# A decoder layer on one core: the weights' preparation spread over the attention turns

## The reference

```python
x = LN(x + self_attention(x))            # 16 query heads, 4 key/value heads, head size 32
x = LN(x + cross_attention(x, ctx))      # 16 heads
amp = sigmoid(x @ amp_w + amp_b)
ph  = tanh(x @ ph_w + ph_b) * pi
h   = (cos(ph) + sin(ph)) * amp
for l in range(2):
    ent = (h @ ent_w[l] + ent_b[l]) @ ent_pw[l] + ent_pb[l]     # 512 -> 2048 -> 512
    h   = LN(h + ent) * g3[l] + b3[l]
    t   = h @ path_w[l][p] + path_b[l][p]                       # p = 0, 1
    h   = LN(h + sum_p t_p * (cos(phase[l][p]) + sin(phase[l][p]))) * g4[l] + b4[l]
out = LN(x + h)
```

## Time and profile before

| | us |
|---|---|
| median of 3 runs | 985.45 (985.22 to 986.75) |
| the profiled execution | 986.26 |
| its span, first to last instruction | 984.4 |
| self attention turns, to about | 258.6 |
| cross attention turns | 258.6 to 512.0 |
| flush, to the first instruction of the fusion phase | 512.0 to 535.4 |
| fusion phase and first gates, to the first drained feed forward unit | 535.4 to 691.2 |
| the rest | 691.2 to 984.4 |

### The profile page before, as it was taken

One profiled execution on the slowest core, in us unless ns is written; L12 is line 12 of the kernel. 1 busy time (PEld: TensorE's weight loads), 2 busy tenths in 40 slices (PEclk: granted clock), 3 DMA queues, 4 the chain that ended last, 5 costly groups with the idle time before them and its releaser, 6 DMA issues. The chain is left out here.

```text
span 984.4 us, 20365 instructions
## 1 busy us (share of the span) xinstructions
PE 891.6 (91%) x5900; PEld 739.3 (75%) x5900; DVE 724.3 (74%) x2072; ACT 528.6 (54%) x1640; POOL 430.6 (44%) x601
## 2 busy tenths in 40 slices
PE   4899999999888999999985987989999999999993
PEld 4788888888777788778864766667778778778672
DVE  3778888888877888888874687892756667657557
ACT  3756665566556666676661333335565564564461
POOL 0234334432222222222231797950664665565466
PEclk9899999999998999999997898999999999999997
DMA  4423332235623543445311764631101101001001
GB/s 148 142 86 109 113 117 89 82 123 166 186 73 109 140 124 95 136 125 139 93 53 41 251 235 161 213 106 65 44 1 43 43 0 43 0 0 43 1 1 43
DMA packets 67045, 92.97 MB, mean 94 GB/s; under 512 B 7216, under 2 KB 41008, under 8 KB 66608
## 3 DMA queue, kind: packets, MB, share of 16 engines
...
## 5 line engine op out<-in xcount | busy, mean ns | idle before, releaser
L675 ACT ACTIVATE prob<-bank,nmax 128x128 f32<-128x128 f32 (+1 forms) x512 | 207.1, 432 | 44.8 <-DVE nmax L734 44.2
L161 PE MATMUL bank<-w_ffn,hT 128*128 128x512 f32 x768 | 193.2, 403 | 0.0
L734 DVE CUSTOM_DVE_ANT_0 bank<-bank,mask 128x128 f32<-128x128 f32 (+1 forms) x512 | 164.1, 392 | 10.8 <-PE bank L895 10.5
L161 PEld LDWEIGHTS bank<-w_ffn,hT 128*128 128x128 f32 x768 | 141.8, 190 | 31.0 <-POOL hT L1366 0.2
L563 POOL TENSOR_SCALAR rwide<-rden 128x256 f32<-128x256 f32 x64 | 26.0, 406 | 275.4 <-DVE rden L745 275.4
L161 PE MATMUL bank<-xT,w_att 128*128 128x256 f32 x864 | 120.8, 293 | 15.4 <-DVE w_att L699 10.5
L161 PEld LDWEIGHTS bank<-xT,w_att 128*128 128x128 f32 x864 | 113.6, 198 | 21.1 <-DVE xT L722 7.0
L161 PE MATMUL bank<-tile 128*128 128x512 f32 x384 | 100.2, 415 | 19.4 <-DVE tile L1177 19.4
L675 ACT ACTIVATION_READ_ACCUMULATOR prob<-bank,nmax 128x1 f32 x512 | 111.6, 218 | 0.0
L907 PE MATMUL bank<-ident,prob 128*128 128x128 f32 x768 | 107.2, 277 | 1.8 <-DVE probT L741 1.4
L1438 ACT ACTIVATE ht<-bank,cols 128x128 f32<-128x128 f32 x192 | 72.3, 457 | 64.2 <-PE bank L1575 64.2
(11 more groups left out here) (119 smaller groups left out, 1472.5 us busy)
## 6 DMA issues: line engine op xcount, KB each, us to landing
q<-stage SPq DMA_DIRECT2D x192, 128.0 KB, 2.3
...
xT_raw<-in_xT SPq DMA_DIRECT2D x8, 512.0 KB, 4.1
xres<-in_x SPq DMA_DIRECT2D x8, 512.0 KB, 3.4
xb<-x SPq DMA_DIRECT2D x8, 512.0 KB, 4.5
aux<-in_path_w SPq DMA_DIRECT2D x8, 512.0 KB, 3.4
```

The lines of the kernel that those rows point to most:

```text
L161: ins = t.matmul(out, lhs(a, k), rhs(b, k), start=first and n == 0 and m == 0, stop=last and n == len(kts) - 1 and m == 2, skip_group_chec ...
L675: ins = s.activation(prob[:, u, c * width:(c + 1) * width], banks[u][:, c * width:(c + 1) * width], ACT.Exp, scale=-1.0, bias=nmax[:, i % ...
L734: ins = v.tensor_tensor_reduce(scored, scored, mask[:, S - width:S], scale=-1.0, scalar=3e38, op0=ALU.add, op1=ALU.min, accum_out=nmax[:, ...
```

## The change

The fusion phase is gone. Its work is in the attention phase:

- The product of the entity weights is cut into 64 units "fu", each for one block of 128 rows of the result and 256 of the 2048 inner columns: 6 matmuls of 512 columns (and one of the identity in the first unit of each sum). They are fillers of the cross turns: ten in the first, nine in each of the next six, none in the last. DVE adds each unit into acc (SBUF). 32 "sp" entries split the rows: ACT the high part (1024 columns), POOL the low, DVE the bias term. The rows come through a ring of three buffers by SP.
- In the last cross turn eight "gs" entries split the gate weights on ACT and POOL.
- The path weights are combined by POOL in the self turns (three operations of 512 columns a turn), after a phase factor made at the start of the kernel and broadcast by DMA.
- Sums, path weights and both attention results go to DRAM ("fd", "x1", "x2") and come back: each turn after the first stores its 512 KB and SP waits for the landing. The feed forward phase loads, splits and uses them; nothing of it is made before its barrier.
- Order inside a step: outputs of group i-2 come first, then for each unit the transposes of group i-1 and the scores of group i. probT and cv have one buffer instead of two. In cross turns ACT copies unit B as well as A. DVE makes the output before the maxima.
- The cross turns and the feed forward blocks are written out instead of looped.

```diff
 def fillers(self, i):
+        elif own == "cross" and after:
+            out[0] += [U, ("cq", 2), U, U]
+            out[1] += [("cv", 0), ("cq", 3), U, ("cv", 1), ("x1t", 0), U, ("x1t", 1)]
+            if wo == "wo":
+                out[1] += [U, ("wo", 0)]
+                out[2] += [("ck", 0), U, ("wo", 1), U, ("cq", 0)]
+                out[3] += [U, ("cq", 1), U, ("ck", 1)]
+            else:
+                out[2] += [("ck", 0), U, ("wout", 0), U, ("cq", 0)]
+                out[3] += [("wout", 1), U, ("cq", 1), U, ("ck", 1)]
         elif own == "cross":
-            out[0] += [("cv", 0), ("cq", 2), ("cv", 1)]
-            out[1] += [("cq", 3)]
+            out[0] += [("cq", 2), ("gs", 0), ("gs", 1)]
+            out[1] += [("cv", 0), ("cq", 3), ("cv", 1), ("gs", 2), ("gs", 3)]
+            out[2] += [("wout", 0), ("gs", 4), ("gs", 5)]
+            out[3] += [("wout", 1), ("gs", 6), ("gs", 7)]
...
# each U becomes ("fu", n), and behind every second one stands the split of a row
+                row = {1: n // 4 * 2 + 3, 3: n // 4 * 2 + 4}.get(n % 4, NL * ET)
+                if row < NL * ET:
+                    told.append(("sp", row))
...
 # PE
+            def fused(t, name):
+                n = name[1]
+                chunk, m = n // KT, n % KT
+                row, cols = 2 * chunk, slice(m * P, (m + 1) * P)
+                starts = chunk % (ET // 2) == 0
+                pr.wait_free(t_, t, name)
+                t_.wait_ge(s_flo, row + 2)
+                bank = pr.tile(t, name, banks)
+                ins = split_products(t_, bank[:, :], lambda h, k: tiles[:, (row + k) % 4, h, 0, cols],
+                                     lambda h, k: tiles[:, (row + k) % 4, h, 1, :], range(2), last=not starts)
...
                 for i in range(t.steps()):
-                    if t.scored(i):
-                        scores(i)
-                    if t.turned(i):
-                        transposes(i - 1, 0)
-                        transposes(i - 1, 1)
                     if t.closed(i):
                         outputs(i - 2)
-                    if t.turned(i):
-                        transposes(i - 1, 2)
+                    if t.scored(i):
+                        kh, qh = stacked(i)
+                    for u in range(U):
+                        if t.turned(i):
+                            transposes(i - 1, u)
+                        if t.scored(i):
+                            scores(i, u, kh, qh)
...
 # ACT
+                            if u in t.copied_by_scalar():
+                                bank = banks[T_BANKS[(U * (i - 1) + u) % 2]]
+                                s.activation(probT[:, 2 * (u - 1):2 * u, P:PW], bank[:, :].rearrange("p (j q) -> p j q", j=2), ACT.Copy).then_inc(s_cp[u], 1)
...
+            def row_hi(row):
+                if row >= 4 and row % 2 == 0:
+                    n = KT * (row // 2 - 2) + KT - 1
+                    pr.wait_full(s, unit_turn[n], ("fu", n))
+                s.wait_ge(s_fraw[row % RR], 32 * (row // RR + 1))
+                s.activation(tiles[:, row % 4, 0, :, :], raw[:, row % RR, :, :], ACT.Copy).then_inc(s_fhi, 1)
...
 # DVE
                 def step(i):
-                    if t.scored(i):
-                        for u in range(U):
-                            maxima(i, u)
-                    if t.turned(i):
-                        probT_tile(i - 1, 1)
-                        reciprocals(i - 1)
                     if t.closed(i):
                         output(i - 2)
-                    if t.turned(i):
-                        probT_tile(i - 1, 2)
+                    for u in range(U):
+                        if t.scored(i):
+                            maxima(i, u)
+                        if u == 0 and t.turned(i):
+                            reciprocals(i - 1)
+                        if u not in t.copied_by_scalar() and t.turned(i):
+                            probT_tile(i - 1, u)
...
 # SP
+            def store(t):
+                wait_alone(q, s_norm, t.lin(TT), s_passed)
+                to = x1_of[t.lin(1, -1)] if t.before == "self" else x2_of[t.lin(1, -1 - B)]
+                q.dma_start(to, xres[:, :, :]).then_inc(s_xo, 16)
+                wait_alone(q, s_xo, t.lin(16), s_passed)
...
 # feed forward phase, ACT
+            k = Banks(s, plan_pro, 0)
+            for i in range(BT):
+                x2T_hi(k, i)
+            gates(k, 0)
+            stage_hi(2)
+            stage_hi(3)
+            s.wait_ge(s_wlo, 2 * NL * KT)
```

836 lines of the change are left out of this document (438 added, 398 removed).

## The result

| | before | after |
|---|---|---|
| device time, median | 986.1 us (985.2 to 988.8, 4 runs) | 1095.8 us (1094.1 to 1101.0, 4 runs) |
| ratio | 1 | 1.112 (1.107 to 1.116) |
| profiled execution | 986.3 us | 1101.0 us |

The forecast was 1011 with a range from 966 to 1037. The direction was right; the size was not: 25 us were forecast and 110 came, outside the range.

What follows compares the result with a forecast made beforehand. PE was taken to bound self turns, PE plus waits for ACT-held banks cross turns. -117.0 + 3.5 + 99.0 + 16.9 + 8 + 10.5 = +20.9, execution 1007.2; with 3.5 for clock, 1011 us, range 966 to 1037.

Steps and rivals of the forecast that it cites:

- Rival 2: Cross turns: units fill the waits, so a turn waits only 2.15 us as before; 963 us (955 to 984), chance 0.22.
- rival 5: Unrolled turns load code, or the feed forward start waits for its DMAs: 5 to 10 us beyond the forecast, chance 0.05.
- its likeliest case: Cross turns: each ACT-drained filler holds its bank, 7.0 us waiting a turn; 1011 us (992 to 1026), chance 0.52.
- I put one back, 3.5: Whole kernel: one low-clock stretch, as in the old second cross turn, adds 3.5 us to the sum.
- rival 3: Cross turns: the clock swings in most turns, five more stretches of 3.5 us; 1028 us, to 1040, chance 0.14.
- 29.25 + 12.5 + 7.0: Steady cross turn: old PE busy time, nine units and waiting make 48.7 us; six turns +99.0.
- the stores and reloads of x1 and x2 lie in SP's idle time: +0: Turns' stores and reloads cost nothing but the last store; 1 to 2 us a turn if a round trip meets a stacking.
- +0.5 a turn: Other self turns: where two short steps follow each other, DVE's copies end just when outputs want them; +3.5 in all.
- +2: Last self turn: 3.5 MB of loads ahead of a stacking, but weights no longer awaited singly; ends -4 and 6.
- +16.9: First cross turn: ten units, 13.9 us, and some 3 us more of waiting.
- +8 and 3.5: Last cross turn: values +1, short first step +1, late gate weights about +6; then SP's wait for the last store, +3.5.
- Rival 4: Cross turns: DVE or POOL becomes the bound, contention or the row ring holding ACT; 3 us a turn, 1032 us, chance 0.07.

Runs made afterwards that it cites:

- sp_order: Changed kernel with only SP's DMAs around the self turns reordered, most loads and the store's wait behind the urgent query stackings: 1063.9 us.
- before_new_order: Kernel before, with only the new order inside a step (outputs first, ACT copying unit B in cross turns), no fu units: 1041.0 us.
- waits_filled: Changed kernel with two products computed twice in each of the six later cross turns, just ahead of waits for banks ACT holds: 1085.8 us.
- best_2: best without SP's wait for POOL's path biases ending the first turn, and with the first cross turn's third row behind two units: 997.4 us.
- units_first: Changed kernel with only the cross turns' fillers reordered, DVE-drained units ahead of the fillers that ACT drains: 1051.0 us.
- short_units: Changed kernel with each unit one matmul instead of six, leaving the entity product incomplete: 1083.9 us.
- best_2_short: best_2 with each unit one matmul instead of six, leaving the entity product incomplete: 1009.8 us.
- best: both, with the old step order in the first seven self turns, one row out of the last, and later gate pieces and x2 load: 999.7 us.
- both: Changed kernel with the edits of sp_order and units_first together, and the last cross turn's gate pieces one step later: 1007.3 us.

## Why the prediction was wrong, point by point

Of the 92 us by which the terms of the sixteen turns were too low, 50 lie in the self turns, where transfers priced at nothing stood ahead of urgent ones (37 us in sp_order), 23 in the six steady cross turns, mostly the clock (17), 12 in the first cross turn and 7 in the last.

**What was right.** The removed phases and the new start of the feed forward part: -117.0, measured -117.0; the first unit is drained 38.75 us behind the first transpose, forecast 38.8. Its mechanism was right as well: the gates end 31.0 us behind the first transpose (forecast 31.7), and DVE's last piece of the weights ends just before the drain. That ACT is at its fillers 6.9 us into a step: 7.05 in the step shown (it starts at 497.92, ACT takes cv at 504.97), 7.44 in before_new_order. The waits of the second and third step, 2.18 and 2.78 for 2.0 and 2.9. PE waited 7.5 us a steady turn, forecast 7.0. PE's work at full clock is 42.4 a turn, forecast 41.75. Rival 2 (963) is excluded, and even the mended filler order ends at 45.4 a turn and not at 43. Of rival 5 the feed forward start did what the forecast said; whether the written-out turns load code at a cost, no run tests. The forecast's own range for its likeliest case does not follow from its terms: their ends, added, reach from 988 to 1036 and not from 992 to 1026. The measured time lies outside both.

**The clock.** The term that failed is "I put one back, 3.5": one stretch at the low clock in the whole kernel, with a chance of 0.14 for "in most turns" (rival 3). It came in most: a clock of 0.91 to 0.97 in five of the six turns and 1.00 in one, 2.8 us a turn, 16.6 in all. That is the larger part of the 23.3 by which the six turns exceed their term; the rest is 0.5 of waiting and 0.65 of work a turn. The forecast had weighed two waits of before, one that kept its speed and one that lost it, and priced the kernel as if the first were the usual case. waits_filled shows that the price is real. The Trainium skill, "TensorE: Matmul & The Clock Gate", section "A second HAM failure mode: psum-queue depth-cycling", says that small idle times between groups of matmuls which go round the banks can make the clock swing. The trace now agrees with it (0.95 over six turns against 1.00 in best_2), though the wait ahead of 521.01 did not bring the clock down, and units_first, with the same banks in another order, shows 0.99.

**The order of a step, in cross turns.** The forecast's term, 29.25 + 12.5 + 7.0, came out near (42.4 busy at full clock and 7.5 waiting), but it does not say what causes what. It priced the order through ACT's 6.9 and let units too short to cover a bank make much of the 7.0. before_new_order has no unit and waits 7.0 as well, so that the agreement is in part luck. Unit length matters as the forecast said, in front of a wait (the third step: 2.78 with a unit, 1.58 without; short_units gave back 1.4 of 10.4 a turn, since the waits grew). What the sum had wrong is that units and waits add: cutting the units does not shorten the turn by their length, and in best_2_short it does not shorten it at all.

**SP's queue in the self turns.** The failing step is "the stores and reloads of x1 and x2 lie in SP's idle time: +0". SP was idle, but the stacking behind it in the queue was not idle work. The trace of before had the price: a stacking of 128 KB lands in 2.3 us, and 1024 KB in 5.6; three loads of 512 KB and a round trip stand ahead of it. sp_order measures it at 37 us over the first eight turns (7.6, 20, 9.3), where the forecast had 4.5 in the first, 2 in the last and nothing in between (its clause of 1 to 2 us a turn would still have been under the 3.3 that came). In the first turn the mechanism was the forecast's: PE waits 6.45 us for the stacking, until 42.7 and not 38. Half speed behind the waits is part of the 37: turns 1 to 6 had a clock of 0.99 and have 0.96, the last self turn has 0.75.

**The order in the self turns.** +0.5 a turn, measured 1.6 (before_new_order), of which the old order gave 0.7 back when the other changes stayed (best). The named mechanism, DVE's copies, is one of two waits of 0.8; the other, for the values that ACT drains, was not in the forecast.

**The last self turn.** +2 was a difference of two guesses. Measured +23.2: 9.3 for SP's queue (sp_order), 1.2 for the order (before_new_order), and 12.7 that remain. The rows' splits and the path on POOL beside DVE are in it (2.96 and 2.61 us where 0.74 and 0.54 are usual); moving one row out and changing the order around it gave 6.4 (best). In both, where SP's queue is mended, PE still waits 9.2 us there for DVE's drains of the output projection, at a clock of 0.87. What of the 12.7 is contention, row work or clock, no run separates: this part stays open.

**First and last cross turn.** +16.9 against +28.8: the order alone is 8.7 of it (43.7 against 35.0), and units first takes 8.5 back; why the order costs more here than in a steady turn was not tested. +8 and 3.5 against 18.2: the wait for the gates' first pieces is there, but they come 16.3 us into the turn and not 12 to 13, and ACT waits 9.8 and PE 11.3 us where some 6 were reckoned. Both moves of the gates together (both, best) took the stretch from 66.7 to 59.1.

**Rival 4** (1032, chance 0.07) is half right: POOL and DVE do stretch each other, but no run shows that DVE's lost time, 0.6 us for each of the 24 bias sums of the six turns, bounds a turn: taking the rows off POOL only moved more work to DVE.
